# Fourier tower and token program: five ky resident, tokens kept on chip, shorter batch-norm chain

## What is computed

```python
def tower(x, p_w, p_b, fw1, fw2, w_w, w_b, bn_g, bn_b, q_w, q_b):
    v = concat([x, gx, gy], -1) @ p_w + p_b                  # lift to 32 channels
    for i in range(4):
        x_ft = rfft2(v)                                      # 12 x 12 modes are kept, at both ends of x
        out_ft[:, :, :12, :12]  = einsum('bixy,ioxy->boxy', x_ft[:, :, :12, :12],  W1[i])
        out_ft[:, :, -12:, :12] = einsum('bixy,ioxy->boxy', x_ft[:, :, -12:, :12], W2[i])
        v = irfft2(out_ft) + einsum('bcxy,cd->bdxy', v, w_w[i]) + w_b[i]
        v = (v - mean(v, (0, 2, 3))) * rsqrt(var(v, (0, 2, 3)) + 1e-5) * bn_g[i] + bn_b[i]
        if i < 3: v = relu(v)
    return einsum('bcxy,cu->bxyu', v, q_w) + q_b

h = tower(...)
h = layernorm(h + attention_encoder(h))                      # 4 layers: linear attention, then a gelu MLP
h = layernorm(h + shared_mlp(h) + top2_experts(h))
```

## Time and profile before

| | before |
|---|---|
| runs, us | 785.52, 787.54, 792.06 (median 787.54) |
| the profiled execution, us | 793.09 |
| its span, first to last instruction, us | 791.3 |
| TensorE busy, us (share of the span) | 645.8 (82%) |
| VectorE busy | 555.0 (70%) |
| ScalarE busy | 359.9 (45%) |
| GpSimd busy | 49.9 (6%) |
| mean granted TensorE clock | 0.931 |
| read from HBM | 24.80 MB |

### The profile page before, as it was taken

One profiled execution on the slowest core, in us unless ns is written; L12 is line 12 of the kernel. 1 busy time (PEld: TensorE's weight loads), 2 busy tenths in 40 slices (PEclk: granted clock), 3 DMA queues, 4 the chain that ended last, 5 costly groups with the idle time before them and its releaser, 6 DMA issues. The chain is left out here.

```text
span 791.3 us, 22405 instructions
## 1 busy us (share of the span) xinstructions
PE 645.8 (82%) x10251; PEld 431.9 (55%) x10251; DVE 555.0 (70%) x802; ACT 359.9 (45%) x485; POOL 49.9 (6%) x88
## 2 busy tenths in 40 slices
PE   3799954767999747669899289998968989898997
PEld 2777731335776513338666133345447878787754
DVE  7768878994589869964798778936218675757462
ACT  0025559500155578000456488635014747474763
POOL 4000000002000000020000000020001111110200
PEclk9999987999699959995999699999989999999999
DMA  8101000013010000040110000130050000000001
GB/s 321 22 22 63 2 1 1 2 41 122 14 52 22 2 0 2 1 161 3 42 42 2 0 2 2 41 122 22 15 193 1 2 1 1 1 2 1 1 1 29
DMA packets 12271, 27.29 MB, mean 34 GB/s; under 512 B 3472, under 2 KB 4368, under 8 KB 12176
## 3 DMA queue, kind: packets, MB, share of 16 engines
q1 hardware_dynamic: 11888, 25.12, 9.4%
q10 hardware_dynamic: 288, 0.73, 0.3%
HBM read 24.80 MB, written 1.05 MB: 33 GB/s over the span
## 5 line engine op out<-in xcount | busy, mean ns | idle before, releaser
L450 ACT ACTIVATE V<-ps,wts 128x1024 f32<-128x1024 f32 x96 | 101.8, 1111 | 242.6 <-PE ps L803 242.6
L624 DVE BATCH_NORM_STATS2 stats<-V 128x6 f32<-128x512 f32 x192 | 117.9, 676 | 16.5 <-ACT V L450 16.5
L500 DVE STREAM_TRANSPOSE A<-V 128x2048 f32<-128x2048 f32 x48 | 107.3, 2275 | 6.7 <-ACT V L399 6.7
L399 ACT ACTIVATE V<-V,small 128x2048 f32<-128x2048 f32 x48 | 96.7, 2083 | 5.0 <-DVE small L652 5.0
L696 PE MATMUL ps<-A,tab 128*128 128x384 f32 x192 | 73.1, 519 | 30.9 <-DVE A L507 30.9
L684 PE MATMUL ps<-A,tab 32*32 32x512 f32 x1536 | 67.2, 646 | 25.4 <-DVE A L500 25.4
L696 PEld LDWEIGHTS ps<-A,tab 128*128 128x128 f32 x192 | 34.9, 195 | 79.1 <-DVE A L507 57.2
L803 PEld LDWEIGHTS ps<-tab,A 64*128 64x128 f32 x1024 | 59.6, 188 | 29.6 <-issue 25.2
L507 DVE STREAM_TRANSPOSE A<-ps 128x1024 f32<-128x1024 f32 x48 | 56.7, 1222 | 20.5 <-PE ps L684 20.5
L618 DVE STREAM_TRANSPOSE A<-ps 128x2048 f32<-128x2048 f32 x24 | 55.6, 2317 | 20.3 <-PE ps L746 20.3
L803 PE MATMUL ps<-tab,A 64*128 64x128 f32 x1024 | 65.8, 278 | 2.0 <-DVE A L618 2.0
(11 more groups left out here) (233 smaller groups left out, 903.3 us busy)
## 6 DMA issues: line engine op xcount, KB each, us to landing
A<-in_modes SPq DMA_DIRECT2D x32, 384.0 KB, 4.3
r_ky<-in_modes SPq DMA_DIRECT2D x16, 384.0 KB, 3.0
wl<-in_layers SPq DMA_DIRECT2D x3, 452.0 KB, 5.8
wm<-in_mixture SPq DMA_DIRECT2D x1, 874.5 KB, 8.1
tab<-in_table SPq DMA_DIRECT2D x1, 656.5 KB, 4.7
A<-in_turned SPq DMA_DIRECT2D x1, 512.0 KB, 3.6
V<-in_pixels SPq DMA_DIRECT2D x4, 128.0 KB
tower_out<-A SPq DMA_DIRECT2D x2, 256.0 KB, 2.9
```

Of the source, the lines that this page charges most:

```text
L399: nc.scalar.activation(pair, pair, ACT.Relu, bias=bias, scale=scale).then_inc(s_relu, 1)
L450: nc.scalar.activation(Vm[:, 2 * h:2 * h + 2, r, 512 * q:512 * (q + 1)], bank(half_of_u(q, r) + 2 * h, 2).rearrange("p (m n) -> p m n", m= ...
L500: nc.vector.transpose(T[n % 3].rearrange("p (k n) -> p k n", k=16), Vk[:, :, P * n:P * (n + 1)]).then_inc(s_T, 1)
L624: last = nc.vector.bn_stats(stats[:, 16 * q + 4 * r + m, :], Vm[:, m, r, 512 * q:512 * (q + 1)])
```

## The change

- RING is 5: ky 4 gets a home in `r_ky` too and is loaded during the inverse transform. Ky 5 and 6 go out behind the y product before the last, and ky 7 to 11 behind the last one, all five at once, with no wait for earlier landings. The places in A change accordingly. To make room, the masks move into A, and the lift weights into MZ by a transfer of their own, so that six constants raise `s_const`.
- A is now a tensor `room` that both programs own. The tower leaves the tokens in its first 1024 columns, and the token program reads them there. The store, its wait and the four loads are gone. The tables `natural` and `centre` are loaded by the tower into the next 256 columns, behind the last mixing matmul; `cst` loses `natural`. Six tensors of the token program lie in the rest of the room.
- `refine` has four steps instead of six, by two fused instructions (a multiply by a column and a second operation in one). The mean is copied out of PSUM with its sign turned, and the two steps for the bias become one.

The core of the diff:

```diff
@@ -114,7 +115,7 @@
-    return table, np.concatenate([grid, last_tables(freq)], axis=1), spectra.reshape(P, 3 * MODES)
+    return table, np.concatenate([grid, last_tables(freq), token_constants()[:, NATURAL:], token_constants()[:, 2 * P:3 * P]], axis=1), spectra.reshape(P, 3 * MODES)
@@ -185,12 +186,19 @@
+KEPT_TOKENS, KEPT_TABLE, KEPT_ALL = 0, 1024, 1280
+ROOM = 8192
+shared = ExitStack()
+rooms = []
...
-    RING = 4
+    RING = 5
@@ -206,17 +214,16 @@
+        A = shared.enter_context(nc.sbuf_tensor("room", [P, ROOM], f32))
+        rooms.append(A)
...
-        A = sb("A", [P, 8192])
...
-        wts = sb("wts", [P, W_TURNED])
+        wts = sb("wts", [P, W_HELD])
...
-        m_pixels = sb("m_pixels", [P, 8 * Q])
-        m_spectra = sb("m_spectra", [P, 48])
@@ -243,8 +250,8 @@
-        place = (3, 4, 0, 1, 2, 5, 6, 7)
-        W = [(r_ky[:, KW * k:KW * (k + 1)] if k < RING else A[:, KW * place[k - RING]:KW * (place[k - RING] + 1)])
+        place = (2048, 2816, 0, 768, 3584, 4352, 5120)
+        W = [(r_ky[:, KW * k:KW * (k + 1)] if k < RING else A[:, place[k - RING]:place[k - RING] + KW])
@@ -256,7 +263,10 @@
-        z_one, g_one, u_out = A[:, 0:768], A[:, 1024:2048], A[:, 2048:3072]
+        z_one, g_one = A[:, 2048:2816], A[:, 3072:4096]
+        u_out, kept_table = A[:, KEPT_TOKENS:KEPT_TABLE], A[:, KEPT_TABLE:KEPT_ALL]
...
+        m_pixels, m_spectra = A[:, 4096:4352], A[:, 4352:4400]
@@ -336,7 +346,8 @@
-            sp.dma_start(wts[:, :], weights[:, 0:W_TURNED]).then_inc(s_const, 16)
+            sp.dma_start(lift, weights[:, W_LIFT:W_CONV]).then_inc(s_const, 16)
+            sp.dma_start(wts[:, :], weights[:, W_CONV:W_TURNED]).then_inc(s_const, 16)
@@ -362,19 +373,17 @@
                 for ky in range(RING + 2, MODES):
-                    if ky >= RING + 5:
-                        sp.wait_ge(s_rload[ky - 3], 16 * (l + 1))
                     load_modes(l, ky)
...
             sp.wait_ge(s_mix, KYP * (L - 1) + 2)
-            sp.dma_start(last_t[:, 0:L_TURNED], grid[:, GRID_ALL:]).then_inc(s_last, 16)
+            sp.dma_start(last_t[:, 0:L_TURNED], grid[:, GRID_ALL:GRID_ALL + L_TURNED]).then_inc(s_last, 16)
             sp.dma_start(last_t[:, L_TURNED:], weights[:, W_TURNED:]).then_inc(s_last, 16)
-            rows = tower_out.rearrange("a (r n) -> (a r) n", r=8)
-            for h, done in enumerate((s_ua, s_uv)):
-                sp.wait_ge(done, 1)
-                sp.dma_start(rows[:, 512 * h:512 * (h + 1)], u_out[:, 512 * h:512 * (h + 1)]).then_inc(s_out, 16)
-            sp.wait_ge(s_out, 32)
+            sp.wait_ge(s_mix, KYP * L)
+            sp.dma_start(kept_table, grid[:, GRID_ALL + L_TURNED:]).then_inc(s_out, 16)
+            sp.wait_ge(s_out, 16)
+            sp.wait_ge(s_ua, 1)
+            sp.wait_ge(s_uv, 1)
 
@@ -527,11 +536,11 @@
-                    link(nc.vector.tensor_tensor(small[:, 12:13], small[:, 11:12], small[:, 11:12], ALU.mult))
-                    link(nc.vector.tensor_tensor(small[:, 13:14], small[:, 12:13], small[:, 9:10], ALU.mult))
+                    link(nc.vector.scalar_tensor_tensor(out=small[:, 13:14], in0=small[:, 11:12], scalar=small[:, 9:10], in1=small[:, 11:12],
+                                                        op0=ALU.mult, op1=ALU.mult))
...
-                    link(nc.vector.tensor_tensor(small[:, 13:14], small[:, 12:13], small[:, 11:12], ALU.mult))
-                    link(nc.vector.tensor_tensor(small[:, 0:1], small[:, 13:14], bn_gain[l], ALU.mult))
+                    link(nc.vector.scalar_tensor_tensor(out=small[:, 0:1], in0=small[:, 12:13], scalar=small[:, 11:12], in1=bn_gain[l],
+                                                        op0=ALU.mult, op1=ALU.mult))
@@ -640,22 +649,22 @@
-                link(nc.vector.tensor_copy(small[:, 5:7], bank(0)[:, 0:2]))
-                link(nc.vector.tensor_tensor(small[:, 7:8], small[:, 2:3], small[:, 5:6], ALU.subtract))
+                link(nc.vector.tensor_scalar(small[:, 5:7], bank(0)[:, 0:2], -1.0, None, ALU.mult))
+                link(nc.vector.tensor_tensor(small[:, 7:8], small[:, 2:3], small[:, 5:6], ALU.add))
...
-                nc.vector.tensor_scalar(small[:, 9:10], bank(1)[:, 0:1], small[:, 6:7], EPS, ALU.add, ALU.add).then_inc(s_bn, 1)
+                nc.vector.tensor_scalar(small[:, 9:10], bank(1)[:, 0:1], small[:, 6:7], EPS, ALU.subtract, ALU.add).then_inc(s_bn, 1)
...
-                link(nc.vector.tensor_tensor(small[:, 12:13], small[:, 0:1], small[:, 5:6], ALU.mult))
-                nc.vector.tensor_tensor(small[:, 1:2], bn_bias[l], small[:, 12:13], ALU.subtract).then_inc(s_norm, 1)
+                nc.vector.scalar_tensor_tensor(out=small[:, 1:2], in0=small[:, 0:1], scalar=small[:, 5:6], in1=bn_bias[l],
+                                               op0=ALU.mult, op1=ALU.add).then_inc(s_norm, 1)
...
-            pe.wait_ge(s_const, 80)
+            pe.wait_ge(s_const, 96)
@@ -1014,13 +1024,18 @@
-        u0 = sb("u0", [P, NX])
-        u0T = sb("u0T", [P, NX])
-        xT = sb("xT", [P, NX])
-        sqT = sb("sqT", [P, NX])
-        h0T = sb("h0T", [P, NX])
-        hT = sb("hT", [P, NX])
-        qs = sb("qs", [P, NX])
+        ctx.callback(shared.close)
+        kept = rooms.pop()
...
+        def in_room(i):
+            return kept[:, KEPT_ALL + NX * i:KEPT_ALL + NX * (i + 1)]
...
+        u0T = in_room(0)
+        xT = in_room(1)
+        sqT = in_room(2)
+        h0T = in_room(3)
+        hT = in_room(4)
+        qs = in_room(5)
@@ -1046,7 +1061,8 @@
-        natural = cst[:, 3 * P + 2 + EXPERTS:]
+        u0, natural, first_centre = (kept[:, a:b] for a, b in ((KEPT_TOKENS, KEPT_TABLE), (KEPT_TABLE, KEPT_TABLE + P),
+                                                               (KEPT_TABLE + P, KEPT_ALL)))
@@ -1173,9 +1188,6 @@
-            for g in range(G):
-                rows = tower_out.rearrange("a (r n) -> (a r) n", r=8)
-                sp.dma_start(part(u0, g), rows[:, GW * g:GW * (g + 1)]).then_inc(s_u[g], 16)
@@ -1202,7 +1214,7 @@
-            nc.scalar.dma_start(cst[:, :], table).then_inc(s_cst, 16)
+            nc.scalar.dma_start(cst[:, :], table[:, 0:NATURAL]).then_inc(s_cst, 16)
@@ -1483,15 +1495,15 @@
-            pe.wait_ge(s_cst, 16)
...
-                pe.wait_ge(s_u[g], 16)
...
-                nc.tensor.matmul(bank(g, 1), centre, part(h0T, g), start=True, stop=True).then_inc(s_ucen, 1)
+                nc.tensor.matmul(bank(g, 1), first_centre, part(h0T, g), start=True, stop=True).then_inc(s_ucen, 1)
...
+            pe.wait_ge(s_cst, 16)
```

21 lines of the change are left out of this document (11 added, 10 removed).

## The result

| | before | after |
|---|---|---|
| median of 20 runs, us | 791.69 | 785.18 |
| ratio to before, 95% interval | | 0.9907 (0.988 to 0.9934) |
| the same, timed once more (12 runs) | | 0.9897 (0.986 to 0.9933) |
| the profiled execution, us; mean granted clock | 793.09; 0.931 | 777.94; 0.949 |

The forecast was 778.0 with a range of 774.0 to 783.5; 785.18 lies above it. Ratios, means and the fit further down leave out executions that a lower clock had lengthened, and the profiled executions of e3, e4 and e8 (mean clock 0.910 to 0.914) are such ones, of which only stages are compared. The profiled execution of after agrees with the forecast to 0.1 us, and that is misleading: among the 20 runs only one was quicker, and its mean clock was among the two highest. So the traces are compared stage by stage here, and the runs by time and clock together.

What follows compares the result with a forecast made beforehand. TensorE, busy 645.8 of 791.3 us, was taken as the bound, with edits paying where it stands still or short-step chains hold all engines. +0.5 - 2.1 - 1.0 - 6.9 = -9.5, so 787.5 - 9.5 = 778.0 us, range 774.0 to 783.5.

Steps and rivals of the forecast that it cites:

- The base: Whole kernel: the terms were taken off a median of 787.5 us for before, not the profiled execution's 793.1.
- The start: Start of the tower: one more transfer ahead of the lift rows delays the path by 0.5 us, bounds 0.3 to 0.6.
- The norms: Batch norm chains: eleven fewer short steps of 0.193 us save 2.1 us, bounds 1.6 to 2.2.
- TensorE waits for that chain too, at 557.68: Last layer's norm: TensorE waits for the refinement chain, so two steps fewer save 0.39 us.
- The loads: Mixing of layer 1: new mode loads save 1.0 of a 2.31 us TensorE stop; bounds 2.3 saved to 1.6 lost.
- quick stretches that make good for a stop: Mixing stages: quick stretches around TensorE's stops largely make them good, so removing a stop gives back less than its length.
- The seam: Between tower and token program: VectorE's first copy moves from 590.40 to 583.5, saving 6.9 us; bounds 5.4 to 7.3.
- I take full clock: Seam: TensorE stands only 1.3 us, so its matmuls run at full clock; at half clock the gain would be 5.4.
- a late start of the token program: Seam rival: late TensorE code, half clock or late constants cut the gain to 5.1 to 5.9, total 779.5; chance 0.22.
- five queued loads that hurt: Mixing rival: five queued loads delay TensorE's code in layers 1 to 3, +4.2 us, total 782.2; chance 0.12.
- a stop wholly gone: Mixing rival: layer 1's stop goes away whole with part of layer 2's, 2.5 us more saved, total 775.5; chance 0.08.
- half-clock stretches that make the token program slower than before: Token program rival: 17 us stretches at 0.50 clock reach into it; two end at 795; chance 0.03.

Runs made afterwards that it cites:

- e3: The changed kernel with three more 128x256 filler matmuls on TensorE behind the centring matmuls at the seam; median 791.2 us, ratio to before 0.9935.
- e4: The changed kernel with all token-program constants loaded by the tower into the room, so nothing at the seam waits for them; 784.6 us, ratio to before 0.9869.
- e8: The changed kernel with mode loads and norms as before, leaving the seam change alone; median 790.3 us, ratio to the kernel before 0.9975.
- e12: The changed kernel unchanged, timed and profiled again; median 786.0 us, ratio to the kernel before 0.9897.
- e1: The changed kernel with mode loads as before (four ky resident, old places, throttle); median 787.1 us, ratio to the kernel before 0.9909.
- e6: The changed kernel with the norm's chain as before, eleven short steps more; median 789.0 us, ratio to the kernel before 0.993.
- e2: The changed kernel with five ky resident but the old waits between loads (ky 10 and 11) back; median 789.0 us, ratio to the kernel before 0.9954.

## Why the prediction was wrong

- **The base** was the largest error. The median of before was 787.54 over three runs and is 791.69 over twenty. Of the 7.2 us between 778.0 and 785.18 this is 4.2; the differences between the kernels (9.5 forecast, 6.5 between the medians, 7.4 by the ratio) are the other 3.0. I noted that the profiled execution lay 5.6 above the median, and took the median as the firmer; the upper end of the range had only 1.3 us for it.
- **The start**, +0.5 forecast: 0.6 on the mean of the eleven profiles. The place was right; that a small delay could put VectorE behind GpSimd on the lift was not seen.
- **The norms**, -2.1 forecast: -1.2. The steps of 0.193 are right, the fused step is not: 0.26 from start to start. My bound for this (0.05 more on each of eleven steps) was near the truth, and I took the other end. The step "TensorE waits for that chain too, at 557.68" failed outright: the row shows a start and no wait, and the fillers ahead of it decide. The last layer gives 0, not 0.39. The other three layers give 0.40 each, not 0.58.
- **The loads**, -1.0 forecast: by size not refuted (0.9 over three layers, each +- 0.8; 0.5 +- 1.6 by the runs). The stops are the fetch of TensorE's code, as was supposed; but that it queues behind the modes, so that a stop goes away with them, is not borne out: the stop of 2.31 us comes back with 0.36 to 2.11 us in profiles of the same changed kernel. A term close to what was measured is luck here. What I had called quick stretches that make good for a stop were stretches at the higher clock.
- **The seam**, -6.9 forecast: -4.3 (the mean of seven, 37.85, against 42.15). Right were the barrier, TensorE's start at 0.53 behind the addition, and that VectorE's wait for the constants is late next. Mis-sized was their landing: 4.4 us and not 3.4. I had named this (half a microsecond more) and had cited the rule for it, but gave the half microsecond only to the range, not to the sum. And the step "I take full clock" failed in six of seven: the clock is full at the first products and falls 7.1 to 8.7 us behind the last addition, where the constants are late, on a chain in which nothing hides it.
- **The sum** of the measured terms is 0.6 - 1.2 - 0.9 - 4.3 = -5.8 us, and the runs at equal clock give -5.3 +- 0.9 (not quite the same measure: the seam's term holds the clock's part there). This was close to the rival "a late start of the token program", in the form in which the constants land late; the gain at the seam was even smaller than its 5.1 to 5.9.
- **The clock** gave something back that no term had: 0.936 on the mean of 27 runs of the changed kernel against 0.928 of 51 runs of before, at 3.7 us per 0.01 some 3 us of the whole gain. Beside the runs of before taken with it, the changed kernel stands 0.007 higher (e12), e1, e4 and e6 0.006 to 0.008, e2 0.001 higher and e8 0.001 lower, each to within 0.004 to 0.007. So the seam alone doesn't seem to raise it (e8), but e2, which is the changed kernel with the throttle, doesn't show the rise either. Which part raises it, or whether the length of the stages merely falls better against the low stretches, stays open.
- Of the rivals, five queued loads that hurt, a stop wholly gone, and half-clock stretches that make the token program slower than before are not borne out; the last had its mechanism right at the seam alone, for 3 us and not for 17.

## What to carry to other kernels

When a chain waits for one small transfer, look at what other queues issue at the same instant, and let them wait for it: here one wait on SP, with weights that are not wanted for 30 us behind it, was worth 3.7 us at the seam and 4.1 us between the medians, nearly as much as the whole edit there. A row that shows when TensorE starts is not a wait for the chain that ends nearby; find what stands ahead of it on its own engine, fillers among it. And take the base from as many runs as the difference needs: with a mean clock that moves a run by 3.7 us for 0.01, three runs are no base for a forecast of 1%.
